# Decoder layer, first stage: sums of the weights on ACT, the residual addition on ACT and POOL, statistics at the end of the step, and the loop written out

## The reference, cut to what matters

```
x = x + attn(layernorm(x))      # first stage of the kernel
x = x + xattn(layernorm(x))     # cross attention with 64 context rows per batch
x = x + ffn(layernorm(x))       # three matrices rounded to -1, 0, 1 times a scale

attn(x):  xn = x / norm(x) * 16 * gamma;  q, kv, a = split(xn @ w_qkva)
          a = sigmoid(a);  h[t] = a[t] * h[t-1] + kv[t];  return q * h
ffn:      scale of a weight = mean(abs(w)), at least 1e-5
```

## Time and profile before

| | |
|---|---|
| median of 3 executions | 529.21 us (528.5 to 530.18) |
| the profiled execution, its own time | 529.48 us |
| span of its profile | 527.7 us |
| PE busy | 479.2 us, 91% of the span |
| DVE busy | 428.0 us, 81% |
| ACT busy | 325.4 us, 62% |
| POOL busy | 304.9 us, 58% |
| mean granted clock of PE | 0.978 |

### The profile page before, as it was taken

The page is one execution under the profiler, slowest core; times in us unless marked ns, Lnnn a source line. Parts: engine busy times, 40 slices in busy tenths (PEclk is TensorE's granted clock), DMA queues, the critical chain, the costliest instruction groups (busy, mean ns, idle before and its releaser), DMA issues.

```text
span 527.7 us, 9241 instructions
## 1 busy us (share of the span) xinstructions
PE 479.2 (91%) x2926; PEld 390.7 (74%) x2954; DVE 428.0 (81%) x936; ACT 325.4 (62%) x450; POOL 304.9 (58%) x482
## 2 busy tenths in 40 slices
PE   1899999989997998999999999999999999998572
PEld 0676787777767887888888888888888888876231
DVE  5899998978526757899999889899898998987672
ACT  4433334146333534688878888888888788784450
POOL 2222232820001477788788788787887887888721
PEclk9989999999999999999999999999999999999786
DMA  8996000240000000011132132312111211212332
GB/s 264 324 343 226 1 0 1 40 81 1 1 1 1 1 1 6 6 26 41 37 55 48 40 47 45 51 36 55 42 46 36 55 43 45 54 38 58 73 90 70
DMA packets 68173, 32.06 MB, mean 61 GB/s; under 512 B 50720, under 2 KB 66336, under 8 KB 68128
## 3 DMA queue, kind: packets, MB, share of 16 engines
q1 hardware_dynamic: 68128, 31.50, 23.8%
HBM read 15.24 MB, written 4.19 MB: 37 GB/s over the span
## 4 chain that ended last, share of the span: by engine, by line
PE 63%; DVE 20%; issue 6%; POOL 5%; DMA 4%; ACT 1%; DVEq 1%; POOLq 0%; ACTq 0%
PE psum L1128 31%; PE psum L1370 9%; PE psum L1375 9%; PE psum L1144 3%; DVE region_a L870 3%; DVE mx L984 2%; DVE region_d L987 2%; PE psum L1348 2%; DMA region_d<-region_d 2%; PE psum L1356 2%; PE psum L1261 2%; PE psum L1231 2%; PE psum L1248 1%; DVE xs L812 1%; DMA region_c<-region_d 1%
## 5 line engine op out<-in xcount | busy, mean ns | idle before, releaser
L523 POOL TENSOR_TENSOR region_d<-region_d,rden 128x1024 f32<-128x1024 f32 x32 | 60.9, 1904 | 80.0 <-DVE rden L1001 79.7
L1128 PE MATMUL psum<-Mhi,xT2hi 128*128 128x260 f32 x256 | 75.0, 293 | 0.2
L1128 PE MATMUL psum<-Mhi,xT2lo 128*128 128x260 f32 x256 | 72.4, 283 | 0.0
L1128 PE MATMUL psum<-Mlo,xT2hi 128*128 128x260 f32 x256 | 72.4, 283 | 0.0
L1370 PE MATMUL psum<-VW,region_d 128*128 128x256 f32 x256 | 61.1, 381 | 4.8 <-DVE pTn L1045 4.8
L1375 PE MATMUL psum<-VW,region_d 128*128 128x256 f32 x256 | 60.5, 379 | 0.0
L1370 PEld LDWEIGHTS psum<-VW,region_d 128*128 128x128 f32 x256 | 48.1, 190 | 14.8 <-DVE pTn L1045 6.2
L1375 PEld LDWEIGHTS psum<-VW,region_d 128*128 128x128 f32 x256 | 48.6, 190 | 6.6
L984 DVE TENSOR_REDUCE mx<-psum 128x8 f32<-128x520 f32 x64 | 44.6, 696 | 10.6 <-PE psum L1128 9.1
L1128 PEld LDWEIGHTS psum<-Mhi,xT2hi 128*128 128x128 f32 x256 | 48.2, 188 | 1.3 <-issue 1.0
L1009 DVE SCALAR_TENSOR_TENSOR region_c<-psum,zw,region_c 128x1024 f32<-128x1024 f32 x32 | 41.0, 1282 | 9.7 <-ACT region_c L693 8.9
(11 more groups left out here) (140 smaller groups left out, 1223.2 us busy)
## 6 DMA issues: line engine op xcount, KB each, us to landing
out_dram<-xs SPq DMA_DIRECT2D x32, 128.0 KB, 1.9
xs<-in_x_dram SPq DMA_DIRECT2D x1, 2560.0 KB, 14.2
VW<-in_L_xattn_Wkv_dram SPq DMA_DIRECT2D x1, 2048.0 KB, 11.9
region_b<-in_L_xattn_Wkv_dram SPq DMA_DIRECT2D x1, 2048.0 KB, 17.4
xs<-in_x_dram SPq DMA_DIRECT2D x3, 512.0 KB, 6.4
region_w<-in_L_ffn_w_gate_dram SPq DMA_DIRECT2D x2, 512.0 KB, 9.6
region_w<-in_L_ffn_w_up_dram SPq DMA_DIRECT2D x2, 512.0 KB, 7.9
region_w<-in_L_ffn_w_down_dram SPq DMA_DIRECT2D x8, 128.0 KB, 5.9
```

The source lines that it names most:

```text
L523: pool.tensor_tensor(p2[:, v, 0:H * MK].rearrange("p (h j) -> p h j", j=MK), e[:, :, 0:MK], rden[:, v, :].unsqueeze(2).broadcast_to([P, H, ...
L1128: mm = pe.matmul(dst, lhsT, rhs, start=i == 0, stop=i == len(terms) - 1)
```

## The change

There are five edits, all in `stage1`:

1. The loop is gone: all steps -2 to 8 are written out (`groups`).
2. The three sums of absolute values move from DVE (a reduction) to ACT: an activation `Abs` with an accumulated output, at the end of steps 1, 2 and 3. The full-size output goes to the place of the rounded weights, which is not yet used.
3. For groups 0 to 4 (`COPIED = 5`) DVE no longer adds `y` to `x`. At the head of its step ACT copies the two PSUM banks to a buffer `yTs` in SBUF, and POOL adds `yTs` to `xs`, behind the power of group g+2 in its queue. The transposes of the next group wait for the copy instead of the addition. Groups 5 to 7 are added as before.
4. DVE's statistics of groups 0 to 4 (`stats2`) come at the end of the step, behind `y1`, and their shift (`shift2`) in the next step, behind the statistics of group g+2. For groups 5 to 7 the order is as before.
5. The sum matmul, `wscale` and `wrecip` move from step 1 to step 5; the transposes that wait for `wscale` are now those of step 6.

```diff
+        yTs = f["kvT"].rearrange("p (t d) -> p t d", t=GT)
+        COPIED = 5
...
+        def groups(step):
+            for g in range(-2, NG + 1):
+                step(g, g % 2)
...
@@ POOL, stage1, behind the power of group g+2
+                if exists(g - 1, COPIED):
+                    pool.wait_ge(yT_copied, g)
+                    rows = xs[:, (g - 1) * GT:g * GT, :]
+                    pool.tensor_tensor(rows, rows, yTs, ALU.add).then_inc(x1_done, 1)
...
@@ ACT
+            def absum_of(i):
+                act.wait_ge(ffn_loaded[i], FFN_LOADS[i])
+                act.activation(tern[i], raw[i], ACT.Abs, accum_out=absum[:, i:i + 1]).then_inc(absum_done, 1)
+
             def stage1(g, u):
                 v = 1 - u
+                if exists(g - 1, COPIED):
+                    act.wait_ge(yT_psum, g)
+                    if positive(g - 1):
+                        act.wait_ge(x1_done, g - 1)
+                    act.activation(yTs, banks(6, 2).rearrange("p b (t d) -> p (b t) d", d=D), ACT.Copy) \
+                        .then_inc(yT_copied, 1)
...
+                if g in (1, 2, 3):
+                    absum_of(g - 1)
@@ DVE
+            def stats2(g):
+                dve.wait_ge(x1_done, g + 1)
+                for t in range(GT):
+                    dve.bn_stats(st2[:, t, :], xs[:, g * GT + t, :]).then_inc(st2_done, 1)
+                for t in range(GT):
+                    dve.wait_ge(st2_done, GT * g + t + 1)
+                    dve.bn_aggr(mv2[:, t, :], st2[:, t, :]).then_inc(mv2_done, 1)
+                dve.wait_ge(mv2_done, GT * (g + 1))
+                dve.tensor_scalar(ve2[:, :], mv2[:, :, 1], 1e-5, None, ALU.add).then_inc(ve2_done, 1)
+            def shift2(g):
+                dve.wait_ge(rstd2_done, g + 1)
+                dve.scalar_tensor_tensor(out=nmr2[:, g * GT:(g + 1) * GT], in0=mv2[:, :, 0], scalar=-1.0,
+                                         in1=rstd2[:, g * GT:(g + 1) * GT], op0=ALU.mult, op1=ALU.mult) \
+                    .then_inc(nmr2_done, 1)
...
-                if exists(g - 1, NG):
-                    rows = xs[:, bass.ds((g - 1) * GT, GT), :]
+                if exists(g - 2, COPIED):
+                    shift2(g - 2)
+                if g - 1 >= COPIED:
+                    rows = xs[:, (g - 1) * GT:g * GT, :]
                     dve.wait_ge(yT_psum, g)
                     dve.tensor_tensor(rows, rows, banks(6, 2).rearrange("p b (t d) -> p (b t) d", d=D), ALU.add) \
                         .then_inc(x1_done, 1)
-                if exists(g - 1, NG):
...
-                if isinstance(g, int) and g == 0:
-                    absum_of(0)
-                    absum_of(1)
-                if isinstance(g, int) and g == 1:
-                    absum_of(2)
...
+                if exists(g - 1, COPIED):
+                    stats2(g - 1)
+                elif exists(g - 1, NG):
+                    shift2(g - 1)
-                if isinstance(g, int) and g == 1:
+                if g == 5:
                     dve.wait_ge(tot_psum, 1)
@@ PE
                     if positive(g - 1):
-                        pe.wait_ge(x1_done, g - 1)
+                        pe.wait_ge(yT_copied if g - 2 < COPIED else x1_done, g - 1)
+                    if g == 6:
                         pe.wait_ge(wscale_done, 1)
...
-                if isinstance(g, int) and g == 1:
+                if g == 5:
                     pe.wait_ge(absum_done, 3)
-                    pe.wait_ge(x1_done, 1)
+                    pe.wait_ge(yT_copied, 5)
```

More of the change, by code:

```diff
@@ L247, in decoder_layer @@
         yT_psum = sem("yT_psum")
+        yT_copied = sem("yT_copied")
         x1_done = sem("x1_done")
@@ L347, in registers @@
             return [value if isinstance(value, int) else eng.to_reg(value) for value in values]
[L349 to L358, removed]
         def exists(n, count):
@@ L381, in batch @@
             return b if isinstance(b, int) else b.with_bounds(min_val=0, max_val=B - 1)
-        S1 = (-2, 2, NG - 2, NG + 1, 2)
+        def groups(step):
+            for g in range(-2, NG + 1):
+                step(g, g % 2)
         def steps(step):
@@ L499, in stage1 @@
                     rounded(2)
-            tiles(pool, stage1, *S1)
+            groups(stage1)
             pool.wait_ge(q_psum, NG)
@@ L618, in _ @@
                 act.activation(w1hi[:, k, :], w1[:, k, :], ACT.Copy, scale=gcol[:, k:k + 1]).then_inc(w1_hi, 1)
-            tiles(act, stage1, *S1)
+            groups(stage1)
             act.preload_act_table(ACT.Exp)
@@ L772, in _ @@
         def _(dve):
[L773 to L777, removed]
             def ternary(i):
@@ L902, in stage1 @@
                     dve.reciprocal(wrecip[:, :], wscale[:, :]).then_inc(wrecip_done, 1)
-            tiles(dve, stage1, *S1)
+            groups(stage1)
             def null_key(k):
@@ L1193, in stage1 @@
                     mm.then_inc(ctxT_psum, 1)
-                if isinstance(g, int) and g == 1:
+                if g == 5:
                     pe.wait_ge(absum_done, 3)
-                    pe.wait_ge(x1_done, 1)
+                    pe.wait_ge(yT_copied, 5)
                     group(bank(6, 3), [(ones[:, :], absum[:, :])]).then_inc(tot_psum, 1)
-            tiles(pe, stage1, *S1)
+            groups(stage1)
             def wq_T(part):
```

## The result

The changed kernel takes 537.47 us (median of 4, 536.95 to 538.16) against 529.69 us (median of 4) beside it: 7.8 us more, a ratio of 1.0146 with a 95% interval of 1.0118 to 1.0174. Forecast were 533.2 us and a range up to 535.6. The direction is right, the forecast of 4.0 us is half of what came, and the time lies outside the range.

The account below looks back on a forecast made before the run. DVE was taken to bound steps 1 to 5, PE's own pace being 10.15 us. Step 6 moves by −3.6 + 5d, +3.9 us at d = 1.5: 533.4, less 0.27 to the median, 533.2 us; range 525.4 to 535.6.

Parts of the forecast that it names:

- Sums of absolute values: Steps 0 and 1: without them on DVE, the transposes of step 1 start at 25.35 us instead of 29.61, 4.26 earlier.
- The last part of x: Start of step 1: DVE reaches group 3's statistics at 25.3 us, the load lands at 26.2, so DVE waits 0.9 us.
- DVE's new step: First stage: DVE's pieces in a row sum to 11.00 us a step without collision, against 10.73 on average before.
- The addition on POOL: Steps 1 to 5: it costs about 1.90 us and starts together with DVE's small chain, which it may delay.
- The delay d: Hold of DVE's small chain by POOL's addition, once in each of steps 1 to 5: 1.5 us taken, at most 1.90.
- The sum: Transposes of step 6 at 81.6 + 5d against 85.22 us; difference −3.6 + 5d, +3.9 us at d = 1.5.
- wscale: Transposes of step 6 wait for it, 2.1 us behind y1; steps 6 and 7 then run as before.
- The rule on the ports: Two-input DVE and SBUF-reading GpSimd instructions exclude each other, first starter keeps the ports; each d would be 1.74 us.
- Rival 3: Full exclusion of DVE's small operation and POOL's addition in each step, d = 1.74: 534.3 us; chance 0.21.
- No collision: Rival: DVE's small operations are not held by POOL's addition, d = 0: 525.6 us, faster; chance 0.23.
- partial collision: Rival: the addition starts late and holds only the small chain's last operation, d about 0.7: 529.1 us; chance 0.14.
- ACT's: Rival: a sum on ACT takes 4 us or more, delaying copy and next sigmoid in steps 2 to 4; chance 0.02.

Follow-up runs that it names:

- Experiment 3: Changed kernel with COPIED = 0: all additions on DVE, statistics in their old place; sums on ACT, written-out loop and wscale in step 5 stay; 524.01 us, ratio 0.9906.
- experiment 6: Kernel before with only the loop of the first stage written out; 530.05 us, ratio 1.0005.
- experiment 2: Changed kernel with POOL's addition in front of the power of the step instead of behind it; 535.38 us, ratio 1.0130.
- experiment 1: Changed kernel with one more wait on POOL: the addition starts only when DVE's small chain of the step has ended; 527.71 us, ratio 0.9968.
- experiment 8: Changed kernel with POOL's second operand being 4 broadcast constants instead of yTs, y of groups 0 to 4 left out of x; one execution, 534.48 us.
- experiment 7: Changed kernel with POOL adding only two of the four tiles of each group, y of the others left out of x; one execution, 531.76 us.
- experiment 4: Changed kernel with wscale and its reciprocal in front of the last statistics of step 5 instead of behind them; 535.2 us, ratio 1.0121.
- experiment 5: On top of experiment 1: DVE's statistics of copied groups moved to the next step, between pw_in and the wait for the power; 522.28 us, ratio 0.9865.

## Why the prediction was wrong

- **Sums of absolute values: right.** L1171 of step 1 starts at 25.69 us (25.35 forecast). Experiment 3 shows the gain in time, 528.76 − 524.01 = 4.75 us, and experiment 6 no part of the loop in it. The sums on ACT cost 2.1 us each and nothing waits for them.
- **The last part of x: right in kind.** DVE waits for it, 0.24 us instead of 0.9, till 25.87 us (26.2 forecast). The start of step 1 differs between executions, from 25.29 us (experiment 2) to 27.43 (experiment 1).
- **DVE's new step: right.** 11.00 us were forecast without the collision; experiment 1 has 10.9 to 11.0, and the changed kernel 13.14 − 2.19 = 10.95 on average.
- **The addition on POOL: the mechanism was right, the size wrong, and this is the step that failed.** The delay d was put at 1.5 us, between "L831 is held" (1.74) and "it slips in, L841 is held" (1.2), and bounded from above by 1.90. It is 2.35 − 0.16 = 2.19 us in each of five steps. Two mistakes make up the difference. First, the small operation does not slip in: POOL starts 0.07 us ahead of it, and it is held. That is 1.74 instead of 1.5. Second, the price of 1.90 us, and with it the upper bound, came from L523, whose second operand is broadcast (experiment 8); with two full operands the addition takes 2.40 us. That is 2.19 instead of 1.74. Five times 0.69 us is 3.45 us.
- **The sum with the measured d.** It would put the transposes of step 6 at 81.6 + 5 x 2.19 = 92.55 us; they start at 91.95, as `x` came 0.33 us earlier and the steps are 0.05 us shorter. The forecast difference would be 3.9 + 3.45 = 7.35 us, close to the measured 7.8. That it comes so close is in part luck: at step 6 the changed kernel is 6.7 us late, step 6 with its slow clock adds 1.65 us, and some 0.9 us of this come back before the end, as the two profiled executions are 7.5 us apart.
- **wscale: right in size.** The transposes of step 6 start 2.1 us behind `y1` (1.86 us of waiting). The forecast that step 6 then runs at 10.15 us held in experiments 1 and 2 and failed in the profiled execution and in experiments 7 and 8, by 1.6 to 1.65 us. How much of this is in the median is not shown. All four executions of the changed kernel have a mean granted clock of 0.973 to 0.978. Among the 19 of the kernel before beside experiments 1 to 4, those at 0.975 took 531.1 to 531.4 us and those at 0.988 took 528.1 to 528.6. So a part of the 7.8 us may be the clock's.
- **The rule on the ports** was set aside because L841 ran beside POOL's power. The Trainium skill, "SBUF — State Buffer", section "Who interferes with whom", says that the instruction that starts first has the shared ports for its whole length. For POOL's additions and DVE's L845 experiments 7 and 8 agree with it. It would have given 534.3 us with my price of the addition, and 533.2 + 3.45 = 536.7 us with the right one. That L841 passed the power of 128 x 4 still stands and is not explained; it was no counterexample for an addition of 128 x 1024. Nor is the power free of such holds: in step 7 of the kernel before, L493 took 1.91 us (99.84 to 101.75) instead of 1.01, having started while DVE's L782 ran (99.66 to 100.88).
- **Rivals.** Rival 3, full exclusion in each step, is what happened, with a longer addition than it was priced with. No collision and partial collision are out (L845 is held in all five steps), and so is ACT's: 2.1 us for a sum.

## What to carry to other kernels

Before an operation moves to POOL, look at which small DVE operations will run at the same moment, not only at POOL's free time: a four-element operation can be held for the whole of POOL's. Here one event, the end of the power, released both, and the collision came in all five steps; a wait that lets the short chain go first removed it. Taking an operation away that covers a wait of its own engine gains time only if something else takes its place in the wait, as the statistics do in experiment 5. And a price is taken from an operation with the same operands: broadcast and full are not the same.

## What the runs showed of the hardware

- POOL's `TENSOR_TENSOR` on 128 x 1024 f32 takes 2.40 us with two full operands and 1.90 us with one broadcast (experiment 8). The 2.40 us are the same while DVE is held (changed kernel), while DVE scans (2.41, experiment 1) and beside DVE's statistics (experiment 2).
- While such an addition runs, DVE's `SCALAR_TENSOR_TENSOR` of 128 x 4 with both inputs in SBUF takes 2.35 us instead of 0.16 (changed kernel), and a one-input `TENSOR_SCALAR` of 128 x 4 takes 1.85 us instead of 0.17 (experiment 2); both end with POOL's operation. `bn_stats` and the aggregates (1.40 and 0.36 us, experiment 2) and the scan, which reads PSUM (2.33 us, experiment 1), keep their times.
- An `Abs` activation of 128 x 2048 f32 with accumulated output takes 1.90 + 0.19 us on ACT (changed kernel), against 2.28 us for the reduction on DVE (kernel before, step 1).
